# Gate projection of a quantised feed-forward stage by Strassen's scheme: seven products for four tiles, on one Trainium2 core

## What is computed

```
x = act_qdq(x)
up = act_qdq(x @ lpbq_dequant(w_up).T)
gate = act_qdq(x @ lpbq_dequant(w_gate).T)
sig = fixed_qdq_u16(jax.nn.sigmoid(gate))
gate = act_qdq(gate * sig)
o = act_qdq(gate * up)
return o @ lpbq_dequant(w_down).T
```

## Time and profile before

| | |
|---|---|
| median of 3 runs | 4807.38 us (4806.02 to 4810.66) |
| the profiled execution: time, span | 4805.85 us, 4803.8 us |
| PE busy over the span | 84% |
| DVE, ACT, POOL busy | 71%, 50%, 54% |
| mean granted clock of TensorE | 0.939 |

### The profile page before, as it was taken

The page is one execution under the profiler, slowest core; times in us unless marked ns, Lnnn a source line. Parts: engine busy times, 40 slices in busy tenths (PEclk is TensorE's granted clock), DMA queues, the critical chain, the costliest instruction groups (busy, mean ns, idle before and its releaser), DMA issues. The chain is left out here.

```text
span 4803.8 us, 50266 instructions
## 1 busy us (share of the span) xinstructions
PE 4028.3 (84%) x15992; PEld 2289.8 (48%) x15992; DVE 3419.7 (71%) x3827; ACT 2409.1 (50%) x4734; POOL 2588.8 (54%) x1527
## 2 busy tenths in 40 slices
PE   7898977799999459989937888888888879978987
PEld 6766875444444124433314555555555543445554
DVE  5654438522377556548878999999999978955677
ACT  1211115322345631127857888888888865423333
POOL 4545965000033011109868999999999976622221
PEclk9999997699999779999969999999999999989999
DMA  3332235232278765435543242242251226710100
GB/s 110 107 103 72 72 112 165 88 105 103 112 275 304 291 262 198 171 108 190 187 180 130 70 140 92 74 162 70 69 180 58 67 86 257 267 60 18 35 27 36
DMA packets 363929, 625.71 MB, mean 130 GB/s; under 512 B 67238, under 2 KB 152647, under 8 KB 351634
## 3 DMA queue, kind: packets, MB, share of 16 engines
q1 hardware_dynamic: 325506, 578.92, 34.5%
q10 hardware_dynamic: 38160, 43.56, 2.5%
HBM read 394.24 MB, written 228.15 MB: 130 GB/s over the span
## 5 line engine op out<-in xcount | busy, mean ns | idle before, releaser
L2315 POOL TENSOR_TENSOR sc_X<-sc_Bm,sc_w 128x1024 f32<-128x1024 f32 x512 | 1192.4, 2364 | 88.5 <-DVE sc_H L2494 64.4
L1375 PE MATMUL ff_ps<-ffn_R,hand_w 128*128 128x512 f32 x1536 | 660.6, 592 | 0.7 <-ACT ffn_R L1414 0.7
L2337 ACT ACTIVATE sc_A<-sc_dt,keep_A 128x1024 f32<-128x1024 f32 x512 | 581.7, 1136 | 83.7 <-DVE sc_Z L2499 63.1
L2367 ACT ACTIVATE sc_hT<-sc_tp,sc_ct 128x128 f32<-128x128 f32 x2048 | 584.6, 375 | 72.5 <-PE sc_tp L2421 69.7
L2421 PE MATMUL sc_tp<-sc_idn,sc_H 128*128 128x128 f32 x2048 | 316.6, 277 | 223.2 <-issue 144.3
L2442 PE MATMUL sc_yp<-sc_Z,sc_idn 128*128 128x512 f32 x1024 | 486.3, 597 | 9.9 <-ACT sc_yo L2373 9.6
L1375 PEld LDWEIGHTS ff_ps<-ffn_R,hand_w 128*128 128x128 f32 x1536 | 291.2, 190 | 364.6 <-issue 362.8
L2421 PEld LDWEIGHTS sc_tp<-sc_idn,sc_H 128*128 128x128 f32 x2048 | 233.6, 141 | 438.6 <-issue 250.7
L2494 DVE TENSOR_TENSOR_SCAN sc_H<-sc_A,sc_X 128x1024 f32<-128x1024 f32 x160 | 358.9, 2273 | 23.9 <-ACT sc_A L2337 12.7
L2494 DVE TENSOR_TENSOR_SCAN sc_H<-sc_A,sc_hc,sc_X 128x1024 f32<-128x1024 f32 x160 | 368.4, 2336 | 2.2 <-ACT sc_A L2337 2.2
L75 POOL TENSOR_TENSOR gp_pbd<-gp_r,ssm_msk 128x512 f32<-128x512 f32 x144 | 182.2, 1265 | 221.2 <-DVE gp_r L478 221.2
(11 more groups left out here) (423 smaller groups left out, 8058.5 us busy)
## 6 DMA issues: line engine op xcount, KB each, us to landing
sc_Bm<-d_xd SPq DMA_DIRECT2D x64, 512.0 KB, 7.4
ffn_gate_d<-ff_o SPq DMA_DIRECT2D x96, 256.0 KB, 2.3
ffn_up_d<-ff_o SPq DMA_DIRECT2D x96, 256.0 KB, 6.3
ffn_g_d<-ff_z SPq DMA_DIRECT2D x24, 1024.0 KB, 6.8
ffn_R<-ffn_up_d SPq DMA_DIRECT2D x22, 1024.0 KB, 13.3
ffn_R<-ffn_g_d SPq DMA_DIRECT2D x19, 1024.0 KB, 10.7
hand_x<-d_x SPq DMA_DIRECT2D x16, 1024.0 KB, 7.3
ff_g<-ffn_gate_d SPq DMA_DIRECT2D x16, 1024.0 KB, 6.3
```

Of the source, the lines that this page charges most:

```text
L1375: last = nc.tensor.matmul(ps[:, 2 + t % 6], w[:, k, h * P:(h + 1) * P], xt[:, n, k], start=(k == 0), stop=(k == KD - 1))
L2315: nc.gpsimd.tensor_tensor(X[:, k % RX], Bm[:, n], w[:, j % 2], ALU.mult).then_inc(db, 1)
L2337: nc.scalar.activation(A[:, k % 2], dt[:, j % 2], ACT.Exp, scale=keepA[:, n:n + 1]).then_inc(ex, 1)
L2367: nc.scalar.activation(hT[:, turned(k) % 2, q], tp[:, b * P:(b + 1) * P], ACT.Copy, scale=ct[:, i % 2, q, n:n + 1]).then_inc(tc, 1)
```

## The change

Two rows of hidden units and two blocks of tokens make a block b of four tiles; splitting the 512 features in two halves makes the product one of 2x2 matrices of 128x256 and 256x512 pieces. Blocks are counted with QH = 6 pairs of rows in each of QP = 4 pairs of token blocks, b = 0 to 23. Block 0 is computed as before (`gate_tile`, 16 matmuls). Each of the others has seven products m1 to m7 of two matmuls each (Strassen's scheme in Winograd's form):

- POOL makes four sums of weight pieces per row pair, 128x256 each (`weight_sums`, 24 in all, kept in `z`), and four sums of token pieces per pair of token blocks, 128x1024 each (`x_sums`, 16 in all, in a ring in the space of `downT`).
- PE runs m1, m3 of the block before, m6, m2, m7, m5, m4 (`block_of_four`). m1, m6 and m7 are added up in one PSUM bank (BP); ACT copies its state after each of the three (`keep_sum`, semaphore `kc`), and PE may add the next only when the copy is made. m2 has bank BS, m4 BR; m5 and then m3 share BQ.
- DVE adds the other products to ACT's copies in `o` (`combine`, PSUM times scale plus `o`, semaphore `cb`), four per block, and then takes the four maxima.
- The x blocks have two buffers (`xb`: `x` and the first half of `g`). The transposes of the next pair of token blocks stand in the blocks with h = 1 and h = 3, in two halves each, after m2 and after m4. Their loads go out two at a time, before the first store of a new pair.
- `downT` is loaded in step 1 of the up phase's loop, since its space is in use before.
- m3 of the last block stands behind the first up tile. The up tiles keep six banks in a ring.

The diff, cut to its core:

```diff
+    QP, QH = NB // 2, HB_ // 2
+    NQB = QP * QH
+    CL = 4
+    BP, BS, BR, BQ = 2, 3, 4, 5
+    S_ORDER = [1, 2, 3, 4, 5, 0]
     with ExitStack() as ctx:
         s = Scope(nc, ctx, "ff")
...
         y = o[:, 0:NU]
-        xin, qa, qb, trd, tev, mm, ev, mxd, mset = [s.sem(n) for n in ("xin", "qa", "qb", "trd", "tev", "mm", "ev", "mxd", "mset")]
+        xb = [x[:], g[:, 0].rearrange("p (a d) -> p a d", a=4)]
+        wsum = z.rearrange("p v t -> p (v t)").rearrange("p (h j k c) -> p h j k c", h=QH, j=4, k=2)
...
+        def quad(b):
+            return divmod(b, QH)
+        def tile_at(t):
+            if t >= NG:
+                return t % NG // HB_, t % HB_
+            p, h = quad(t // 4)
+            if t < CL:
+                return divmod(t, 2)
+            return 2 * p + (t % 4 in (1, 3)), 2 * h + (t % 4 in (1, 2))
+        def after_m(name, b):
+            return {"m1": (mp, 3 * b - 2), "m6": (mp, 3 * b - 1), "m7": (mp, 3 * b), "m2": (ms, b), "m4": (mr, b),
+                    "m5": (mq, 2 * b - 1), "m3": (mq, 2 * b)}[name]
...
+        def turned(b):
+            p, h = quad(b)
+            return 2 * p + 2 + h // 2 if h in (1, 3) and p + 1 < QP else None
+        def x_slot(p, j):
+            return (4 * p + j) % 6
         def first(i):
...
+                    sp.wait_ge(trd, 1 + (n - 1) * KD)
+                sp.dma_start(xb[n % 2], xr[n]).then_inc(xin[n % 2], 16)
             def store_tile(t):
-                n, h = t % NG // HB_, t % HB_
+                n, h = tile_at(t)
                 dst = gate_d if t < NG else up_d
                 sp.wait_ge(mxd, 1 + t + 1)
...
-                    load_x(n + 2)
-                for h in range(HB_):
-                    store_tile(n * HB_ + h)
...
+            for b in range(NQB):
+                p, h = quad(b)
+                if h == 0 and p + 1 < QP:
+                    load_x(2 * p + 2)
+                    load_x(2 * p + 3)
+                for r in range(4):
+                    store_tile(4 * b + r)
...
+                    sp.wait_ge(mq, 1 + 2 * (NQB - 1))
+                    sp.dma_start(downT[:], ffn_t[2]).then_inc(dnl, 16)
                 if i == 3:
...
+            def weight_sums(h):
+                n = 4 * S_ORDER.index(h)
+                a11, a12 = [gateT[:, 2 * k:2 * k + 2, 2 * h * P:(2 * h + 1) * P] for k in range(2)]
+                a21, a22 = [gateT[:, 2 * k:2 * k + 2, (2 * h + 1) * P:(2 * h + 2) * P] for k in range(2)]
+                s1, s2_, s3, s4 = [wsum[:, h, j] for j in range(4)]
+                nc.gpsimd.tensor_tensor(s1, a21, a22, ALU.add).then_inc(ws, 1)
+                nc.gpsimd.tensor_tensor(s3, a11, a21, ALU.subtract).then_inc(ws, 1)
+                pool.wait_ge(ws, 1 + n + 1)
+                nc.gpsimd.tensor_tensor(s2_, s1, a11, ALU.subtract).then_inc(ws, 1)
+                pool.wait_ge(ws, 1 + n + 3)
+                nc.gpsimd.tensor_tensor(s4, a12, s2_, ALU.subtract).then_inc(ws, 1)
+            def x_sums(p):
+                b11, b21 = xt[:, 2 * p, 0:2], xt[:, 2 * p, 2:4]
+                b12, b22 = xt[:, 2 * p + 1, 0:2], xt[:, 2 * p + 1, 2:4]
+                t1, t2, t3, t4 = [xsum[:, x_slot(p, j)] for j in range(4)]
+                pool.wait_ge(tev, 1 + (2 * p + 2) * KD)
+                for j, (out, l, r) in enumerate(((t1, b12, b11), (t2, b22, t1), (t3, b22, b12), (t4, t2, b21))):
+                    q = 4 * p + j - 6
+                    if q >= 0:
+                        sem, count = after_m(("m5", "m6", "m7", "m4")[q % 4], q // 4 * QH + QH - 1)
+                        pool.wait_ge(sem, 1 + count)
+                    if j == 1:
+                        pool.wait_ge(xs, 1 + 4 * p + 1)
+                    if j == 3:
+                        pool.wait_ge(xs, 1 + 4 * p + 2)
+                    nc.gpsimd.tensor_tensor(out, l, r, ALU.subtract).then_inc(xs, 1)
...
+            for h in S_ORDER[1:]:
+                weight_sums(h)
+            for p in range(1, QP):
+                x_sums(p)
             gs.pool_part(nc, pool)
             for i in range(NT_):
...
+            def third(b):
+                pe.wait_ge(cb, combined(b, 1))
+                times(BQ, wsums(b, 3), tokens(b, 1, 1), True, mq)
+            def free(b, r):
+                if b > 1:
+                    pe.wait_ge(cb, combined(b - 1, r))
+            def block_of_four(b):
+                p, h = quad(b)
+                if b > 1:
+                    pe.wait_ge(kc, 1 + 3 * (b - 1))
+                else:
+                    pe.wait_ge(ev, 1 + 1)
                 if h == 0:
-                    pe.wait_ge(tev, 1 + (n + 1) * KD)
-                pe.wait_ge(ev, 1 + max(t - 5, 0))
-                for k in range(KD):
-                    last = nc.tensor.matmul(ps[:, 2 + t % 6], w[:, k, h * P:(h + 1) * P], xt[:, n, k], start=(k == 0), stop=(k == KD - 1))
-                last.then_inc(mm, 1)
-
-            transposes(0)
-            for n in range(NB):
-                for h in range(HB_):
-                    project(n * HB_ + h)
-                    if h == 5 and n + 1 < NB:
-                        transposes(n + 1)
-            for t in range(NG, 2 * NG):
-                project(t)
-
-            pe.wait_ge(ev, 1 + 2 * NG)
+                    pe.wait_ge(tev, 1 + (2 * p + 2) * KD)
+                times(BP, quarter(b, 0, 0), tokens(b, 0, 0), False, mp)
+                if b > 1:
+                    third(b - 1)
+                pe.wait_ge(kc, 1 + 3 * (b - 1) + 1)
+                times(BP, wsums(b, 1), xsums(b, 1), True, mp)
+                free(b, 0)
+                if b == 1:
+                    pe.wait_ge(ev, 1 + 2)
+                times(BS, quarter(b, 0, 1), tokens(b, 1, 0), False, ms)
+                if turned(b) is not None:
+                    transposes(turned(b), (0, 1))
+                pe.wait_ge(kc, 1 + 3 * (b - 1) + 2)
+                times(BP, wsums(b, 2), xsums(b, 2), True, mp)
+                free(b, 3)
+                if b == 1:
+                    pe.wait_ge(ev, 1 + 4)
+                times(BQ, wsums(b, 0), xsums(b, 0), False, mq)
+                free(b, 2)
+                times(BR, quarter(b, 1, 1), xsums(b, 3), False, mr)
+                if turned(b) is not None:
+                    transposes(turned(b), (2, 3))
+            transposes(0, range(KD))
+            gate_tile(0)
+            transposes(1, range(KD))
...
+            def keep_sum(b, name, r):
+                t = 4 * b + r
+                sem, count = after_m(name, b)
+                act.wait_ge(sem, 1 + count)
+                act.wait_ge(st[t % NO], 1 + t // NO * 16)
+                nc.scalar.activation(o[:, t % NO], ps[:, BP], ACT.Copy, scale=xs_s).then_inc(kc, 1)
...
+            def combine(b, r):
+                t = 4 * b + r
+                name, bank, other, scale = (("m2", BS, 0, xs_s), ("m5", BQ, 2, xs_s), ("m4", BR, 2, nxs[:]), ("m3", BQ, 3, xs_s))[r]
+                sem, count = after_m(name, b)
+                dve.wait_ge(sem, 1 + count)
+                dve.wait_ge(kc, 1 + 3 * (b - 1) + (1, 3, 3, 2)[r])
+                if r == 1:
+                    dve.wait_ge(st[t % NO], 1 + t // NO * 16)
+                nc.vector.scalar_tensor_tensor(out=o[:, t % NO], in0=ps[:, bank], scalar=scale, in1=o[:, (4 * b + other) % NO],
+                                               op0=ALU.mult, op1=ALU.add).then_inc(cb, 1)
...
-                    largest(n * HB_ + h)
-                    if h == 3 and n + 1 < NB:
-                        round_x(n + 1)
+            nc.vector.tensor_scalar(nxs[:], xs_s, -1.0, None, ALU.mult).then_inc(nx, 1)
+            round_x(1)
+            for t in range(CL):
+                largest(t)
+            round_x(2)
+            dve.wait_ge(nx, 2)
+            for b in range(1, NQB):
+                if b > 1:
+                    combine(b - 1, 3)
+                    largest(4 * b - 2)
+                combine(b, 0)
+                if b > 1:
+                    largest(4 * b - 1)
+                combine(b, 1)
+                largest(4 * b)
+                combine(b, 2)
+                largest(4 * b + 1)
+                if b + 1 < NQB and turned(b + 1) is not None and turned(b + 1) > 2:
+                    round_x(turned(b + 1))
+            combine(NQB - 1, 3)
+            largest(NG - 2)
+            largest(NG - 1)
```

More of the change, by code:

```diff
@@ L1358, in _, with transposes @@
         def _(pe):
[L1359 to L1360 removed]
+            def transposes(n, ks):
+                for k in ks:
                     j = n * KD + k
@@ L1378, in _, with gate_tile @@
-            transposes(0)
-            for n in range(NB):
-                for h in range(HB_):
-                    project(n * HB_ + h)
-                    if h == 5 and n + 1 < NB:
-                        transposes(n + 1)
-            for t in range(NG, 2 * NG):
-                project(t)
-            pe.wait_ge(ev, 1 + 2 * NG)
+            def gate_tile(t):
+                n, h = tile_at(t)
+                pe.wait_ge(tev, 1 + (n + 1) * KD)
```

(28 more changed lines are left out.)

86 lines of the change are left out of this document (57 added, 29 removed).

## The result

The changed kernel takes **4767.1 us** (median of four runs, 4764.4 to 4771.3) where the kernel before took 4806.7 on the same chip: a ratio of 0.991, interval 0.990 to 0.992, some 40 us less. The prediction was 4769.5, range 4763 to 4784. The profiled execution took 4764.4 us, span 4762.6.

What follows compares the result with a forecast made beforehand. The prediction took TensorE to bound the gate and up projections. Its terms, -39.5 - 2.8 + 1.1 + 1.6 + 1.7 = -37.9 us, took the median of 4807.4 to 4769.5 us, range 4763 to 4784.

Steps and rivals of the forecast that it cites:

- Matmuls: Gate projection: 23 blocks of four tiles need 7 x 2 instead of 16 matmuls, 46 fewer at 0.858 us, -39.5 us.
- Transposes: Gate projection: six of eight transpose groups are cut in two with products between, hiding PE's wait for ACT's copy, -2.8 us.
- Block 1: Gate block 1: no m3 stands ahead of its m6, so PE waits for ACT's copy of m1, +1.1 us.
- Start: Gate start: GpSimd's first weight sums delay VectorE's four roundings and the third transpose group, +1.6 us, bounds 0 and 2.8.
- Hand-over: Gate to up projection: the gate scale comes 5.8 us later against PE, which waits before up tile 7, +1.7 us.
- Cover of 0.59 us, 45 times: Gate blocks: one product (1.72 us) covers each 1.13 us copy of the shared bank, 0.59 us to spare, 45 times.
- Rival 3: Gate products: bubbles of 0.13 us, or copies overrunning their cover by 0.45 us 45 times, give 4790 us; chance 0.09.
- Store wait: Gate blocks: m6's copy needs an earlier store, allowed 4.3 us; no cost, even with paired x loads at blocks 6 and 12.
- rival 5: Gate blocks: stores beyond 4.3 us stop PE in 22 blocks; no gain from 6.0 us, 4818 at 6.5; chance 0.06.
- Rival 2: Gate projection: doubled x loads land late, so rounding stops PE 4.9 us, twice, giving 4779 us; chance 0.13.
- Up phase: Up projection: the loop has 23 us before PE's end, so 4 to 6 us more lateness doesn't matter.
- rival 4: Up projection: the loop behind the later scale becomes last and the end stays, 4805 us; needs 23 us of lateness; chance 0.04.

## Why the prediction was right, step by step

- **Matmuls, -39.5.** Right. 92 records fewer; block 6 lasted the 12.02 us of the prediction (m1 at 1015.48, the next m1 at 1027.50), and half of m4 taken out gave its 0.86 a block back once the waits are counted.
- **Transposes, -2.8: mis-sized, -4.2.** The twelve halves took 10.6 us (ten at 0.87, those in blocks 7 and 13 a little more) where six groups took 14.8. I took only the wait for ACT's copy away, and left each half the 1.0 us that eight records had; between products a half takes less.
- **Block 1, +1.1: 1.04**, but with wrong parts. The prediction had 0.31 us until ACT reads, 0.69 for the copy and 0.13 for the restart. In block 1 ACT began at 954.48, 0.19 after m1 was through, and PE restarted 0.05 after the copy: 0.93. The 0.31 came from the first tile, whose own late weights (0.10) it holds: ACT's copy there began 0.20 us after PE's next matmul did (at 939.93). Left out was the 0.10 that m6 loses to late weights, and the errors nearly cancel.
- **Start, +1.6: 1.34**, and it vanished when the sums stood behind the roundings. The third transpose group began 4.78 us after the first rounding, for 5.05 forecast. That this is so near is partly luck, since the engines did not take strict turns. The fourth rounding ended 4.73 us after the first began (2.87 before), so 1.9 later where my list had 2.1; but the list had three sums in that time, and all four were done. Strict turns of the four roundings (2.87) and four sums (0.72 each when alone) would take about 5.8 us. The rule of the Trainium skill, "SBUF — State Buffer", "Who interferes with whom", held for which instructions meet: the roundings and sums shown above slow one another, while the 12 sums of DVE from PSUM and SBUF that ran beside a sum of GpSimd took 751 ns and the others 750 (743 in the earlier trace rows), and its maxima 678 and 677. It did not hold for how much: that page of the Trainium skill lets one engine keep the ports for a whole instruction, and here about 5.8 us of such instructions went by in 4.73.
- **Hand-over, +1.7: 1.3** (1.23 and the 0.10 of late weights), gone in the kernel with m3 first.
- **Moved `downT` load, 0.** Right; it landed in 13.6 us, and a second one cost nothing that shows.
- **Cover of 0.59 us, 45 times.** It held, with more room than forecast (1.72 less 0.93 is 0.79): no wait in blocks 2 to 23 for a copy that began on time, and without the product one that costs 1.04 in each block. Rival 3 is out.
- **Store wait.** The budget of 4.3 us held in the ordinary blocks: the gate stores landed in 2.0 (median), so rival 5 is out. In blocks 7 and 13 the step was mis-sized. I had the two x loads landed at T+16.8, 8 us after they went out, and the store of tile 4b+1 at T+17.5, 1.6 us ahead of its deadline at T+19.1. In the changed kernel (T = 1015.48) the loads went out at T+8.8 as forecast, but the second landed at T+17.8, and the store 1.3 us behind it, at T+19.1. ACT's copy of m6 began then:

```profile
1034.61 0.69 ACT L1596 ACTIVATE ff_o<-ff_ps,hand_scx 128x512 f32<-128x512 f32 x1 [4.50 <-DMA ffn_gate_d<-ff_o]
```

  PE lost only 0.2 us to it in block 7 (0.11 of waiting, 0.10 for late weights), but the room was 0 and not 1.6: in the other profiles of kernels with the same loads PE waits 0 to 1.2 us here. Rival 2 named the wrong partner (the rounding, done by T+17) at the right place and for the right cause.
- **Up phase.** The loop ended 23.0 us before PE, as it did before, so rival 4 is out. But this isn't the spare time that the prediction read into it. All fourteen profiles have 23.0 us there, though the first reload was rounded 9 us after PE's last gate matmul in the kernel before and 11.2 to 14.9 us after it in the others. Near its end the loop waits for the up tiles, as in this row of the changed kernel, and ACT's copies wait for PE. How much lateness the loop could have borne is not shown.

```profile
1541.81 0.69 DVE L1707 TENSOR_REDUCE ff_amu<-ff_o 128x1 f32<-128x512 f32 x1 [2.75 <-ACT ff_o L1588]
```

The terms as measured, -39.5 - 4.2 + 1.04 + 1.34 + 1.3 and 0.2 for late weights behind the stores, give -39.8; the stage's own clock shows -39.6. The first tile, 3.5 us in both profiles, adds nothing. The error of the sum is thus 1.4 us of transposes and 0.7 of the small waits, less 0.2. Of the 2.4 us between 4769.5 and 4767.1 a further 0.7 is that the kernel before had a median of 4806.7 this time and not 4807.4, which is within what differs from run to run.
